# Attention pass of an audio tower: score products over all 128 rows, with keys that GpSimd sets apart by head

## The reference, cut to what matters

```python
def _L1_attn_ref(x, w_qkv, b_qkv, w_proj, b_proj):
    NUM_HEADS = 12
    ...
    qkv = jnp.einsum('bnc,oc->bno', fake_quant(x), fake_quant(w_qkv)) + b_qkv
    qkv = qkv.reshape(B, N, 3, H, hd).transpose(2, 0, 3, 1, 4)
    q, k, v = (qkv[0], qkv[1], qkv[2])
    attn = jnp.einsum('bhnd,bhmd->bhnm', fake_quant(q), fake_quant(k)) * scale
    attn = jax.nn.softmax(attn, axis=-1)
    out = jnp.einsum('bhnm,bhmd->bhnd', fake_quant(attn), fake_quant(v))
    out = out.transpose(0, 2, 1, 3).reshape(B, N, C)
    out = jnp.einsum('bnc,oc->bno', fake_quant(out), fake_quant(w_proj)) + b_proj
    return out
```

## Time and profile before

| | us |
|---|---|
| median of 3 runs | 4510.53 |
| lowest and highest | 4503.53, 4511.26 |
| the profiled execution's own time | 4503.24 |
| its span in the profile | 4501.5 |
| TensorE, VectorE, ScalarE, GpSimd busy | 3654.4, 3363.6, 2562.8, 1774.6 |

### The profile page before, as it was taken

One profiled execution on the slowest core, in us unless ns is written; L12 is line 12 of the kernel. 1 busy time (PEld: TensorE's weight loads), 2 busy tenths in 40 slices (PEclk: granted clock), 3 DMA queues, 4 the chain that ended last, 5 costly groups with the idle time before them and its releaser, 6 DMA issues. The chain is left out here.

```text
span 4501.5 us, 71192 instructions
## 1 busy us (share of the span) xinstructions
PE 3654.4 (81%) x23492; PEld 2805.5 (62%) x23540; DVE 3363.6 (75%) x6250; ACT 2562.8 (57%) x5049; POOL 1774.6 (39%) x2209
## 2 busy tenths in 40 slices
PE   0069999998499999999996668888688864459999
PEld 0059999998499999999995421111122224459999
DVE  7948888887567777777767679999777765645555
ACT  4645555553344444444444679999788864424433
POOL 5757777776133333333330022222100012434444
PEclk9999999999699999999996655555555555569999
DMA  4335455454322222122224681000111111334442
GB/s 115 99 103 141 138 143 136 131 148 115 101 84 90 90 90 76 66 83 90 87 87 115 221 322 32 24 24 24 43 44 44 44 47 58 91 107 126 130 117 85
DMA packets 271288, 439.77 MB, mean 98 GB/s; under 512 B 46458, under 2 KB 207978, under 8 KB 260078
## 3 DMA queue, kind: packets, MB, share of 16 engines
q1 hardware_dynamic: 249518, 410.06, 29.6%
q0 software_dynamic: 20480, 25.87, 2.0%
q10 hardware_dynamic: 1024, 0.54, 0.0%
HBM read 328.24 MB, written 117.16 MB: 99 GB/s over the span
## 5 line engine op out<-in xcount | busy, mean ns | idle before, releaser
L1101 POOL TENSOR_TENSOR c_ap<-c_ac,c_ap 128x420 fp32r<-128x420 f32 x340 | 406.0, 1194 | 759.3 <-ACT c_ap L1260 759.3
L726 PE MATMUL b_pA<-ab_woutT,b_ys 128*105 128x192 f32 x3840 | 689.2, 326 | 1.2 <-ACT b_ho L646 0.4
L726 PEld LDWEIGHTS b_pA<-ab_woutT,b_ys 128*105 128x105 f32 x3840 | 610.3, 171 | 12.1 <-ACT b_ho L646 3.9
L564 POOL TENSOR_TENSOR b_ys<-b_hs,b_cb 128x525 f32<-128x525 f32 x384 | 506.9, 1320 | 221.7 <-DVE b_hs L791 179.7
L1985 DVE TENSOR_REDUCE g_raw<-g_pS 128x1 f32<-128x525 f32 x816 | 549.5, 703 | 31.7 <-PE g_pS L1940 30.4
L1961 ACT ACTIVATE g_pS<-g_pS,g_stt 128x525 f32<-128x525 f32 x816 | 553.7, 776 | 20.0 <-POOL g_stt L1914 19.1
L1940 PE MATMUL g_pS<-g_qk 16*128 16x262 bf16 (+1 forms) x1536 | 461.6, 408 | 94.3 <-ACT g_pS L1961 36.1
L791 DVE TENSOR_TENSOR_SCAN b_hs<-b_ae,b_pB 128x525 f32<-128x525 f32 x384 | 479.3, 1248 | 41.2 <-ACT b_ae L665 7.3
L1260 ACT ACTIVATE c_ap<-c_ac 128x420 fp32r<-128x420 f32 x340 | 189.3, 557 | 558.0 <-DVE c_ac L1427 556.3
L1169 PE MATMUL c_pD<-cw_wd,c_ap 128*105 128x192 f32 x4080 | 438.3, 257 | 27.1 <-POOL c_ap L1101 27.1
L1169 PEld LDWEIGHTS c_pD<-cw_wd,c_ap 128*105 128x105 f32 x4080 | 423.7, 171 | 51.3 <-POOL c_ap L1101 38.2
(11 more groups left out here) (387 smaller groups left out, 7977.4 us busy)
## 6 DMA issues: line engine op xcount, KB each, us to landing
b_cb<-dram_ct SPq DMA_DIRECT2D x64, 1050.0 KB, 5.9
c_wb<-dram_wt SPq DMA_DIRECT2D x60, 840.0 KB, 9.7
b_cb<-dram_ct SPq DMA_DIRECT2D x64, 525.0 KB
dram_slots<-g_empty SPq DMA_DIRECT2D x32, 772.0 KB, 21.2
c_wb<-dram_wt SPq DMA_DIRECT2D x20, 1050.0 KB, 6.4
o_xr<-dram_slots SPq DMA_DIRECT2D x64, 258.0 KB, 4.7
dram_qk<-f_qk SPq DMA_DIRECT2D x16, 787.5 KB
g_qk<-dram_qk SPq DMA_DIRECT2D x16, 787.5 KB, 4.2
```

The source lines that it names most:

```text
L564: pool.tensor_tensor(ys[:, u % RING, :], hs[:, u % RING, :], cb[:, g % 3, u % GU, :], ALU.mult).then_inc(s["ys"], 1)
L726: ins = pe.matmul(into, ys[:, u % RING, t * TP:(t + 1) * TP], woutT[:, u % NU, :], start=(u == 0 and t % 2 == 0), stop=(u % NU == NU - 1), ...
L1101: nc.gpsimd.tensor_tensor(ap[LO][:, r, :], ac[:, r, :], ap[HI][:, r, :].bitcast(F32), ALU.subtract)\
```

## The change

For m < 4 a score product no longer takes the 19 rows of its head from qk, for both operands. The stationary operand comes from a new buffer kb with 128 rows: one unit u = 4g + m of it holds the 128 keys of block m four times, once for each head, with zeros in the rows of the other heads. The moving operand is all 128 rows of the group's queries. kb has KR = 3 slots. GpSimd makes a unit with one product of the keys with the mask of the heads, 128 x 4 x 128 elements. There are NK = 12 units in a batch. TensorE waits for the unit ("kb"), and GpSimd waits, before it writes a slot again, for the last fill that has used it ("S").

```diff
+        KR, NK = 3, HG * 4
+        kb = sb("kb", [128, KR, 4, 128], BF16)
...
+        def last_fill(u):
+
+            return (u // 4 * NT + u % 4 * 4 + 3) // 3
...
+            def keys_apart(b, k, u):
+                if u >= KR:
+                    pool.wait_ge(s["S"], at(b, TN, last_fill(u - KR) + 1))
+                elif b:
+                    pool.wait_ge(s["S"], at(b - 1, TN, last_fill(u + NK - KR) + 1))
+                g, m = divmod(u, 4)
+                shape = [128, 4, 128]
+                x = qk[:, k, HG + g, m * 128:(m + 1) * 128]
+                pool.tensor_tensor(kb[:, u % KR, :, :], x.rearrange("p (a l) -> p a l", a=1).broadcast_to(shape),
+                                   mask[:, :].rearrange("p (j b) -> p j b", b=1).broadcast_to(shape), ALU.mult)\
+                    .then_inc(s["kb"], 1)
+
             def body(b, i, k, last):
                 pool.wait_ge(s_in[k], i * 16 + 16)
+                for u in range(KR):
+                    keys_apart(b, k, u)
                 pool.wait_ge(s["S"], at(b, TN, -TN))
                 pool.wait_ge(s["R"], at(b, HG, -HG))
                 blocks(pool, kt[:, k, :, :, 0:QR], qk[:, k, HG:2 * HG, QM:S], mask).then_inc(s["kt"], 1)
                 pool.wait_ge(s["qa"], at(b, HG, HG))
                 blocks(pool, qr[:, k, :, :, :], qk[:, k, 0:HG, QM:S], mask).then_inc(s["qr"], 1)
+                for u in range(KR, NK):
+                    keys_apart(b, k, u)
...
                     if m < 4:
-                        at_ = slice(HP * j, HP * j + HD + 3)
-                        ins = pe.matmul(into, qk[at_, k, HG + g, m * 128:(m + 1) * 128], qk[at_, k, g, 0:QM],
-                                        start=True, stop=True)
+                        u = 4 * g + m
+                        pe.wait_ge(s["kb"], at(b, NK, u + 1))
+                        ins = pe.matmul(into, kb[:, u % KR, j, :], qk[:, k, g, 0:QM], start=True, stop=True)
```

More of the change, by code:

```diff
@@ L2026, in attention_heads @@
         s = {n: sem("q_" + n) for n in ("A", "T", "qa", "kt", "qr", "S", "E", "P", "AV", "AVg", "ev", "R", "Er", "Pr", "Rv",
-                                        "rev", "om")}
+                                        "rev", "om", "kb")}
         block = ctx.enter_context(nc.Block())
@@ L2077, in _ @@
         def _(pool):
-            for n in ("kt", "qr"):
+            for n in ("kt", "qr", "kb"):
                 pool.sem_inc(s[n], CREDIT)
```

## The result

| | before | after |
|---|---|---|
| median of 3 runs, us | 4510.53 | 4538.55 |
| lowest and highest | 4503.53, 4511.26 | 4538.12, 4549.46 |
| profiled execution, its span | 4503.24, 4501.5 | 4549.46, 4547.8 |
| VectorE, GpSimd busy in the span | 3363.6, 1774.6 | 3459.4, 2021.3 |

The changed kernel is slower by 28.0 us, a ratio of 1.0075 with a 95% interval of 1.0056 to 1.0094. The forecast was +25.

The account below looks back on a forecast made before the run. ScalarE bounds the batch before, VectorE after: 22.3 us work, 6.3 waiting for GpSimd and 1.3 other waits make 29.9 against 28.4; 16 x 1.5 plus 1 at the start gives +25, 4535 us, range 4515 to 4570.

Parts of the forecast that it names:

- The clock rises: Attention pass: TensorE's granted clock rises from 0.50 (1.2 GHz) in the first batch and holds, as 128 rows are used.
- the rival with a swinging clock: Attention pass: the clock goes up and down, 4560 to 4620 us; chance 0.10 together with a clock that stays low.
- TensorE is not the bound: Attention pass at the raised clock: TensorE needs some 18 us of a 28 us batch.
- A unit takes 1.03 us: GpSimd's product making one unit of keys: 1.03 us, kept range 0.85 to 1.27, 12 a batch.
- the f32 price: GpSimd's units at 1.27 us each: +80 us, so 4590; chance 0.10 together with a key supply that limits.
- The two take turns, 6.3 us a batch: VectorE and GpSimd exclude each other in SBUF: 8.5 of 12 units cost VectorE 0.74 us each, 6.3 a batch.
- VectorE idles 1.3 us a batch: Attention pass: waits VectorE can't lose, before the copy of pO and other short ones, about 1.3 us a batch.
- The start, +1 us: Start of the attention pass: the first fill waits for GpSimd's first unit of keys, adding 1 us.
- The sum: VectorE's batch, 29.9 us against 28.4, times 16, plus the start: +25 us, 4535 against the median.
- GpSimd stays hidden: Attention pass: units fall into VectorE's gaps and the clock's gain is kept, 4483 or 4456 us; chance of faster 0.25.
- The clock stays at 1.2 GHz: Attention pass: TensorE needs 38 us a batch, +154 us, about 4660; chance 0.10 together with a swinging clock.
- TensorE waits for keys: Three-slot ring: supply decides only if a unit takes over 2.3 us with its wait; part of a case at 0.10.

Follow-up runs that it names:

- e6_six_slots: The changed kernel with six slots of kb instead of three; 4544.32 us, ratio 1.0073 to the kernel before.
- e12_changed_again: The changed kernel itself, unaltered, run once more beside the kernel before on the same chip; 4550.79 us, ratio 1.0070.
- e1_keys_once: The changed kernel making only the first three units, in batch 0, so all later products read old keys; 4467.34 us, ratio 0.990.
- e3_dma_keys: The changed kernel with keys set apart by transfers into a kb of all 12 units instead of by GpSimd; 4461.28 us, ratio 0.9892.
- e4_one_strip: The kernel before, its three 19-row score products all taken from the first strip, one behind the other; 4687.20 us, ratio 1.0394.

## Why the prediction was right, step by step

- **The clock rises.** Right. It was 0.50 for the first fills (3225 to 3235 us) and up from 3237 on. That it falls again for a while in about every second batch stood only in the rival with a swinging clock, at 4560 to 4620. It cost much less: the pass of 485.2 us is 5 us longer than 16 batches of 29.99.
- **TensorE is not the bound.** Right, though it was busy for 22.4 us of a batch at full clock where the sum had 18. e6_six_slots and the one wait of 1.8 us for keys show that supply isn't either.
- **A unit takes 1.03 us.** The least of 192 is 1032 ns. The length worked out from two bf16 rows held to 1% (the slope, 1.63 ns, to 3%); the f32 price (1.27), and with it the rival at 4590, fell. So did the estimate of 1.3 us by the Trainium skill's "GPSIMD Engine Reference", section on elementwise cycle accounting: the trace has 1.03, and 1.68 ns an element where 2.6 cycles at 1.2 GHz are 2.17.
- **The two take turns, 6.3 us a batch.** VectorE's busy time went from 22.3 to 28.3 us, so 6.0 of waits. The product of the two factors was right, its placing was not: by the groups the roundings took 4.2 us of it ((325.9 - 258.6)/16), prr 1.2 and the constants' cast and product 1.2 (together 6.6, as instructions overlap a little in this sum), where I had it all on the roundings. The constants' product, whose two operands lie in SBUF and which the prediction doesn't name among the instructions that collide, went from a mean of 278 to 732 ns. My factors (8.5 paid units of 0.74) were never measured apart, and in the runs with smaller units the same rule gave a quarter too much and more (4.5 for 3.6, 2.6 for 1.5). That their product fits the whole unit within 0.3 us is in part luck. One reading under them was off as well: in the earlier trace rows GpSimd's product begins at 3419.08, ahead of the rounding at 3419.10 and not just after it, so which of the two came first there can't be told from these starts; the ends are as read.
- **VectorE idles 1.3 us a batch.** This term was mis-sized. In batches at full clock it is 29.99 - 28.81 = 1.2, and the batch of 29.99 us is the 29.9 of the sum. In the others it is 3.1, and the mean over the pass is (485.1 - 453.2)/16 = 2.0.
- **The start, +1 us.** It was +2.0. TensorE's wait before its first fill went from 0.6 us (for VectorE) to 1.8 (for the unit), 1.2 more; and the exponential began 0.65 us after the first score product before and 1.48 after, since three 128-row products follow each other while the clock is still at 0.50. That second term was left out.
- **The sum.** 30.6 us in the pass and 2.0 at its start, 32.6 in the profiled execution, for 16 x 1.5 + 1 = 25. Between the medians it is 28.0, with an interval of 25 to 42 by the ratio, and 31.6 in e12_changed_again.

Of the rivals, the best case of "GpSimd stays hidden", no collisions at all, is what e1_keys_once and e3_dma_keys measure, 25.6 and 25.5 us a batch for its 25.0; it did not come about since the units don't fall into the gaps. "The clock stays at 1.2 GHz" fell at the first page. "TensorE waits for keys" fell with e6_six_slots.

## What to carry to other kernels

An engine that is busy for a sixteenth of a stretch isn't free to take work: before giving a neighbour's copy or product to GpSimd, look whether VectorE's instructions there are of the kind whose duration grows when the two meet (compare one that starts alone with one that starts behind GpSimd), and price the work in VectorE's time, which here was half its own length. A gain on an engine that stops being the bound is not there to be set against the cost on the one that becomes it; price both edits alone and then the sum of each engine. Zero rows that only fill up a product can pay through the clock, if laying them out is cheap: here by transfers (1.1% under the kernel before) or by VectorE itself (0.7%), and not by GpSimd.

## What the runs showed of the hardware

- With 19 rows in use TensorE was granted 0.50 at 0.96 busy (e4_one_strip), with 128 rows, most of them zeros in the stationary operand, 1.00 at 0.87 busy (e1_keys_once).
- A GpSimd memset of 1026 ns, which reads nothing, lengthened VectorE's roundings to a mean of 1240 ns from 959, as much as a product of the same length.
- Three 128-row score products at 2.4 GHz take longer than three 19-row ones side by side at 1.2 GHz. In the last rows of the changed kernel's timeline above the combination starts 0.74 us behind the scores (3474.87 to 3475.61), where it was 0.54, and the next scores 1.18 us behind these, where a fill was 1.08. So the clock gives nothing back in a fill as such. By ScalarE's waits in e3_dma_keys (31 us, 72 before) its gain lies in the rests and in what stands behind a copy of pO.
